# Degrees, row normalisation and table scaling of a graph layer, two stages written as one

## The chip, the cores and the metric

The kernel runs on one core of a Trainium2 chip. The metric is the device time of one execution in microseconds. The kernel computes one graph layer in stages that follow one another; this document is about two neighbouring ones.

## The reference, cut to what matters

12,500 nodes with 256 features, 200,000 weighted edges. The part that the change touches:

```python
xn = _layernorm(x, axis=-1)                     # (x - mean) / sqrt(var + 1e-5)
deg = segment_sum(ew_sl, row_sl, num_segments=N)   # edge weights by source node, self loops of weight 1
dinv = where(deg > 0, rsqrt(deg), 0.0)
norm = dinv[row_sl] * ew_sl * dinv[col_sl]
h7 = segment_sum((xn @ W)[col_sl] * norm[:, None], row_sl, num_segments=N) + b
...                                             # two dense layers on h7, an attention branch, a top-2 mixture of experts
```

The kernel gathers rows of a table `dinv * xn` first and multiplies by W afterwards. It also needs `xn` itself and `x + xn` (the skip rows). So between the sorting of the edges and the gathering stand: the weighted degree of each node, the normalisation of each row, and the scaling of each row by its node's `dinv`.

## The kernel before, in words

Nodes lie in 98 blocks of 128; a block of normalised rows is one 128 x 256 tile in `k.acc`, which holds all 98. An earlier phase has sorted the edges into 1664 tiles of 128 edges, each of which belongs to one block; a record is a packed word (target node, place of the source node within its block, `loc`) and the edge weight. Blocks are taken in order of their edge counts; `k.perm` says which block of nodes stands at place n, so SyncE loads one register of it for each DMA on x or the table (`natural`, line 182).

`degrees_and_rows` (from line 927) does two things side by side.

Its start (lines 1068 to 1101): SyncE loads the two halves of the records, VectorE adds them, TensorE turns them so that a tile's edges lie on partitions, ScalarE copies them to `k.recs`, and VectorE cuts `loc` out and splits the weight into three bf16 pieces whose sum is exact.

Then a loop of 13 trips of 128 tiles, in eight batches of 16. In each batch VectorE makes a one-hot of `loc` for each edge, 128 columns a tile (L1105, two instructions of 8 tiles), and TensorE multiplies: the one-hot as weights, the three pieces as three columns (L1177). After a trip the three columns are added (L1138), turned (L1163), copied (L1038) and added up by block with a matrix that says which tile belongs to which block (L1167). The total degree is complete when the last trip is through. The first trip and the last two are written out; trips 1 to 10 are a loop on the engines, in which addresses come from registers.

Beside each batch one block of x is normalised: SyncE loads it into a ring of four (L999), VectorE takes statistics (L1118, L1123), ScalarE the root (L1045), VectorE reciprocal and shift (L1128, L1130), and ScalarE writes `xn` to `k.acc` (L1048) and the skip rows to a ring of four (L1055). SyncE stores both (L1007, L1009) and loads the next block, all in one queue in program order. GpSimd only makes a row of numbers.

`scale_table` (from line 1192) begins after a barrier: roots and reciprocals of all 98 x 128 degrees, then ScalarE scales four and VectorE three of every seven blocks in `k.acc` in place (L1230, L1257), and SyncE stores each block to the table as soon as its seven are scaled (L1217), one register load and one DMA of 128 KB each. The bias of the layer is cut into three bf16 pieces beside it. `k.phase_done()` between phases clears the semaphores and makes all engines meet.

## Time and profile before

| | us |
|---|---|
| median of three runs (4654.85 to 4659.12) | 4658.87 |
| the profiled execution, its own time | 4660.25 |
| its span, first to last instruction | 4658.5 |
| the two stages: from the records' load to the gather stage's first instruction | 363.4 |

Over the whole span TensorE is busy 76%, VectorE 65%, GpSimd 58% and ScalarE 33%. The largest groups belong to the gather stage, which begins at 1166 us, and to the experts at the end. The page's forty slices are 116 us long; the two stages lie in slices seven to ten. A row of the timeline gives the start, the length of a merged run of equal instructions, the engine (SPq is SyncE's DMA queue), the line, what is written and read, the count, and in brackets the idle time before it and what ended that. Means in a row of groups are from start to write, and neighbours on one engine overlap by a part of it.

### The profile page before, as it was taken

To read this page: it belongs to the slowest core of one execution; us is meant where nothing else is said; L and a number is where in the kernel's file an instruction comes from. 1 tells how busy PE (TensorE), PEld (TensorE's weight loads), DVE (VectorE), ACT (ScalarE), POOL (GpSimd) and SP (SyncE) were. 2 spreads that over 40 slices of the span, in tenths; PEclk is the share of its full clock that TensorE was granted. 3 is DMA by queue.
4 is the path that set the end of the run, shared out by engine and by line. 5 is a ranking of instruction groups with operands and counts; after the bars stand their busy time and mean duration, and the time that the engine had idled before them with its cause. 6 is when DMAs were issued, how large, how long until landed. Compare 5 with 4: busy or idle time off the path is not lost. (4 is left out here: it accounts for less than half of the span.)

```text
span 4658.5 us, 80245 instructions
## 1 busy us (share of the span) xinstructions
PE 3532.4 (76%) x20196; PEld 2666.5 (57%) x20196; DVE 3032.5 (65%) x7684; ACT 1516.5 (33%) x4675; POOL 2709.1 (58%) x2419
## 2 busy tenths in 40 slices
PE   7777775791677777877765778777777679999986
PEld 6445543570344444444443666665666469999885
DVE  8899997883555655655554555555555675555566
ACT  2455553663111111111100322222222255555442
POOL 0488887000666666666666666666666325555553
PEclk9677787555888887888877888888898789999998
DMA  2111112454333333333333444444445712222456
GB/s 73 3 3 3 3 3 36 133 166 142 110 110 109 109 108 110 112 109 110 111 102 92 132 133 131 127 132 130 133 132 124 155 37 71 67 69 69 142 198 220
DMA packets 297683, 472.63 MB, mean 101 GB/s; under 512 B 97283, under 2 KB 195850, under 8 KB 297615
## 3 DMA queue, kind: packets, MB, share of 16 engines
q0 software_dynamic: 140544, 273.69, 23.8%
q1 hardware_dynamic: 149919, 194.17, 12.4%
q10 hardware_dynamic: 7154, 3.99, 0.3%
q8 instruction: 28, 0.46, 0.0%
q14 instruction: 38, 0.31, 0.0%
HBM read 350.37 MB, written 123.70 MB: 102 GB/s over the span
## 5 line engine op out<-in xcount | busy, mean ns | idle before, releaser
L1483 POOL DMA_INDIRECT rows<-table,idx x1664 | 1688.0, 1014 | 799.1 <-issue 466.4
L1764 DVE TENSOR_TENSOR acc<-acc,ps_seg 128x256 f32 x1664 | 697.1, 419 | 939.0 <-remote 669.2
L1929 PE MATMUL ps_seg<-rows,pick 128*128 128x256 f32 x3328 | 955.4, 419 | 129.6 <-issue 63.6
L1929 PEld LDWEIGHTS ps_seg<-rows,pick 128*128 128x128 f32 x3328 | 654.7, 208 | 355.1 <-issue 241.8
L756 POOL DMA_INDIRECT records<-sort_rec,sort_addr x280 | 527.6, 1884 | 262.0 <-DVE sort_rec L859 159.4
L1608 DVE TENSOR_SCALAR pick<-iota_row,loc,ewt 128x128 f32<-128x128 f32 x1680 | 530.3, 362 | 3.9
L1801 PE MATMUL ps_kv<-wkv,xT 128*128 128x512 f32 x392 | 264.5, 811 | 246.5 <-ACT xT L1506 149.1
L2367 POOL DMA_INDIRECT y_rows<-arena,idx x212 | 256.1, 1208 | 293.8 <-DVE arena L2414 235.7
L2499 PE MATMUL ps_h<-arena,up_now 128*128 128x128 f32 x3392 | 420.6, 278 | 0.0
L2483 PE MATMUL ps_y<-down_now,arena 128*128 128x256 f32 x1696 | 402.7, 381 | 0.0
L2499 PEld LDWEIGHTS ps_h<-arena,up_now 128*128 128x128 f32 x3392 | 401.2, 194 | 1.8 <-issue 0.3
L911 PE MATMUL ps_out<-acc 128*128 128x240 bf16 x1568 | 278.7, 362 | 143.7 <-DVE acc L845 143.6
L778 ACT ACTIVATE sort_others<-ps_rank,sort_own 128x98 f32<-128x98 f32 x840 | 272.9, 375 | 287.2 <-PE ps_rank L891 175.8
L2483 PEld LDWEIGHTS ps_y<-down_now,arena 128*128 128x128 f32 x1696 | 307.6, 191 | 33.3
L911 PEld LDWEIGHTS ps_out<-acc 128*128 128x128 bf16 x1568 | 200.8, 131 | 208.8 <-DVE acc L845 139.9
L2394 ACT ACTIVATE arena<-ps_h,up_now 128x128 f32<-128x128 f32 x848 | 241.7, 368 | 221.3 <-PE ps_h L2499 221.3
L2357 POOL DMA_INDIRECT arena<-ffn_rows,idx x212 | 223.7, 1055 | 141.9 <-DVE idx L2407 74.3
L1801 PEld LDWEIGHTS ps_kv<-wkv,xT 128*128 128x128 f32 x392 | 88.9, 243 | 343.6 <-issue 177.5
L2414 DVE TENSOR_TENSOR arena<-ps_y,down_now 128x256 f32<-128x256 f32 x212 | 90.0, 425 | 285.4 <-PE ps_y L2483 200.1
L2382 ACT ACTIVATE arena<-ps_x,gb 128x128 f32<-128x128 f32 x424 | 171.0, 453 | 208.5 <-issue 108.6
L1177 PE MATMUL ps_rows_tile_deg<-rows_ew,rows_at_node 128*128 (+1 forms) x1664 | 189.7, 180 | 49.6 <-DVE rows_at_node L1105 43.5
L845 DVE TENSOR_TENSOR acc<-sort_in_slot,sort_piece 128x3360 bf16<-128x3360 bf16 x112 | 208.8, 1907 | 7.0
(380 smaller groups left out, 5372.9 us busy)
## 6 DMA issues: line engine op xcount, KB each, us to landing
rows<-table,idx POOLq DMA_INDIRECT x1664
acc<-y_rows SPq DMA_DIRECT2D x28, 640.0 KB
rows_x<-in_x SPq DMA_DIRECT2D x100, 128.0 KB
xn<-xn_dram SPq DMA_DIRECT2D x100, 128.0 KB
xn_dram<-acc SPq DMA_DIRECT2D x98, 128.0 KB
skip_dram<-rows_skip SPq DMA_DIRECT2D x98, 128.0 KB
table<-acc SPq DMA_DIRECT2D x98, 128.0 KB
xT_dram<-xT SPq DMA_DIRECT2D x98, 128.0 KB
```

The source lines that it names most:

```text
L756: pool.indirect_dma_start(out=k.granules[h], out_offset=bass.IndirectOffsetOnAxis(addr[:, h, g:g + 1], 0), in_=rec[:, h, g * GRANULE:(g + ...
L778: last = act.activation(others[:, (m + h) % 2, :], ps_rank[g][:, at:at + BLOCKS], ACT.Relu, bias=own[:, :], accum_out=q[:, m:m + 1])
L911: last = pe.matmul(OUT, in_lane[:, h, c, :], valued[:, h, side, :, at, :], start=(c == 0), stop=(c == LOT - 1))
L1483: pool.indirect_dma_start(out=rows[:, t, :], out_offset=None, in_=k.table, in_offset=bass.IndirectOffsetOnAxis(idx[:, h, t:t + 1], 0), bou ...
L1608: dve.tensor_scalar(pick[:, h, t, :], k.iota_row[:, :], loc[:, h, t:t + 1], ewt[:, h, t:t + 1], ALU.is_equal, ALU.mult).then_inc(picked[t], 1)
L1764: dve.tensor_tensor(here, here, sums(u), ALU.add).then_inc(added[u], 1)
L1801: pe.matmul(ps_kv[:, :], xT[:, q, c, :], k.wkv[:, c, :], start=(c == 0), stop=False)
L1929: pe.matmul(sums(t), pick[:, h, t, :], rows[:, t, :], start=True, stop=True).then_inc(summed_up[t], 1)
L2367: pool.indirect_dma_start(out=k.y_rows, out_offset=bass.IndirectOffsetOnAxis(idx[:, u, 1:2], 0), in_=y[:, u % 2, :], in_offset=None, bound ...
L2394: act.activation(hT[:, slot, c * P:(c + 1) * P], ps_h[slot][:, c * P:(c + 1) * P], ACT.Gelu, bias=parts[slot][1][:, c:c + 1]).then_inc(gel ...
L2483: last = pe.matmul(ps_y[slot][:, 0:D], hT[:, slot, c * P:(c + 1) * P], parts[slot][2][:, c, :], start=(c == 0), stop=(c == HC - 1))
L2499: last = pe.matmul(ps_h[slot][:, c * P:(c + 1) * P], parts[slot][0][:, d, c * P:(c + 1) * P], xT[:, slot, d * P:(d + 1) * P], start=(d == ...
```

## The change

The two functions become one, `degrees_rows_table`, without a barrier between them, and no engine loops: everything is written out.

- Degrees. `loc` is cut into a high part (4 values) and a low part (32). For a group of 64 tiles VectorE makes one-hots of 4 columns and of 32, and multiplies the 4-column one by the three weight pieces, 12 columns a tile. TensorE takes the 32-column one-hot as weights and the 12 columns as the other operand: the result is 32 partitions x 12 columns a tile, in four PSUM banks, and VectorE adds the three pieces (`keep`). After two groups four small matmuls bring these 4 x 32 rows into the layout of 128 (`gather`), ScalarE copies them, and TensorE multiplies by that trip's tile-to-block matrix (`add`); VectorE adds the result to `deg`, which starts at 1.
- The tile-to-block matrices are made one trip at a time.
- Rows. Blocks are normalised in chunks of four: 25 chunks, x in a ring of three chunks, skip rows in a ring of two. `1/std + 1` is taken by VectorE instead of ScalarE. Two chunks are normalised before the records' copies, five more before the first group; group g then goes with chunk g + 7. Statistics are taken one chunk ahead.
- Table. As edges are sorted by block, the blocks up to `READY[j + 1]` have their whole degree after trip j. Their roots, reciprocals and scaling (half on ScalarE, half on VectorE) and their stores follow inside the loop, some six groups behind.
- SyncE: xn and skip rows are stored four blocks at a time; x and table still one block a DMA, with the registers of a chunk loaded by one instruction (`naturals`).
- The weight pieces are written twice each as pairs, by ScalarE instead of VectorE; the bias is cut at the very start.

Of the diff stand here the added lines that matter for the order of the work; what they replace is printed above, and is gone as a whole.

```diff
+            def naturals(eng, n, count):
+                _, values = nc.values_load_multi_w_load_instructions(
+                    k.perm[0:1, n:n + count], engines=[eng.engine], min_val=0, max_val=BLOCKS - 1,
+                    skip_runtime_bounds_check_because="blocks are numbered below BLOCKS")
+                return values
+            k.natural, k.naturals = natural, naturals
...
-                degrees_and_rows(k)
-                k.phase_done()
-                scale_table(k)
+                degrees_rows_table(k)
...
+    GROUP = P // 2
+    GROUPS_T = 2 * TRIPS
+    NORM = 4
+    NORMS = -(-BLOCKS // NORM)
+    LEAD = 7
+    EARLY = 2
+    X_CHUNKS = 3
...
+    HIGH, LOW = P // 32, 32
+    EW_PIECES = 3
+    WIDE = EW_PIECES * HIGH
+    HALF_BANK = GROUP // 2
+    READY = [BLOCKS * P * j // TILES_USED for j in range(TRIPS)] + [BLOCKS]
...
-        DEG = ps_deg[:, 0:BLOCKS]
+        DEG = [ps_T[r][:, 0:BLOCKS] for r in range(2)]
...
+                def load(c):
+                    for u, at in enumerate(k.naturals(sp, NORM * c, len(blocks_of(c)))):
+                        sp.dma_start(x[:, c % X_CHUNKS, u:u + 1, :], x_blocks[:, bass.ds(at, 1), :]).then_inc(
+                            x_in[c % X_CHUNKS], 16)
+                def put(c):
+                    b = blocks_of(c)
+                    start_after(sp, xn_out[c % X_CHUNKS], 16 * (c // X_CHUNKS))
+                    sp.wait_ge(xn_done, b.stop)
+                    sp.dma_start(xn_blocks[:, b.start:b.stop, :], k.acc[:, b.start:b.stop, :]).then_inc(xn_out[c % X_CHUNKS], 16)
+                    sp.wait_ge(skip_done, b.stop)
+                    sp.dma_start(skip_blocks[:, b.start:b.stop, :], skip[:, c % 2, 0:len(b), :]).then_inc(skip_out[c % 2], 16)
+                def put_table(j):
+                    at = k.naturals(sp, READY[j], len(ready(j)))
+                    sp.wait_ge(act_scaled, act_total(j))
+                    sp.wait_ge(dve_scaled, dve_total(j))
+                    for u, n in enumerate(ready(j)):
+                        sp.dma_start(table_blocks[:, bass.ds(at[u], 1), :], k.acc[:, n:n + 1, :]).then_inc(table_out, 16)
+                for c in range(X_CHUNKS):
+                    load(c)
+                sp.wait_ge(bias_cut, 2 * BIAS_PIECES)
+                sp.dma_start(k.bias3[:, :], pieces[0:1, :, :]).then_inc(bias_put, 16)
+                tabled = 0
+                for c in range(NORMS):
+                    put(c)
+                    if c + X_CHUNKS < NORMS:
+                        load(c + X_CHUNKS)
+                    g = c - LEAD
+                    if g >= 7 and g % 2 == 1:
+                        put_table(tabled)
+                        tabled += 1
+                for j in range(tabled, TRIPS):
+                    put_table(j)
...
+                def normalised(c):
+                    act.wait_ge(shift_done, c + 1)
...
+                    for u, n in enumerate(blocks_of(c)):
+                        act.activation(k.acc[:, n, :], x[:, c % X_CHUNKS, u, :], ACT.Identity, scale=rstd[:, n:n + 1],
+                                       bias=shift[:, n:n + 1]).then_inc(xn_done, 1)
+                    act.wait_ge(up_done, c + 1)
+                    start_after(act, skip_out[c % 2], 16 * (c // 2))
+                    for u, n in enumerate(blocks_of(c)):
+                        act.activation(skip[:, c % 2, u, :], x[:, c % X_CHUNKS, u, :], ACT.Identity, scale=up1[:, n:n + 1],
+                                       bias=shift[:, n:n + 1]).then_inc(skip_done, 1)
...
+                for c in range(EARLY):
+                    deviations(c)
+                    normalised(c)
                 for n, (w, g) in enumerate(turns):
                     act.wait_ge(turned, n + 1)
                     to = k.recs[:, g * P:span(g).stop * P, w]
                     act.activation(to if w == 0 else to.bitcast(F32), ps_T[n % 2][:, 0:P * len(span(g))],
                                    ACT.Identity).then_inc(unturned, 1)
+                act.wait_ge(unturned, len(turns))
+                piece(0, ew)
+                act.wait_ge(rest_done, 2)
+                piece(1, rest)
+                for c in range(EARLY, EARLY + 2):
+                    deviations(c)
+                act.wait_ge(rest_done, 4)
+                piece(2, rest2)
+                for c in range(EARLY, EARLY + 2):
+                    normalised(c)
+                for c in range(EARLY + 2, LEAD):
+                    deviations(c)
+                    normalised(c)
+                deviations(LEAD)
...
+                    if c + 1 < NORMS:
+                        deviations(c + 1)
+                    if g >= 3 and g % 2 == 1 and (g - 3) // 2 < TRIPS:
+                        keep_sums((g - 3) // 2)
+                    if g >= 5 and g % 2 == 1 and (g - 5) // 2 < TRIPS:
+                        roots((g - 5) // 2)
+                    if c < NORMS:
+                        normalised(c)
+                    if g >= 6 and g % 2 == 0 and (g - 6) // 2 < TRIPS:
+                        scaled((g - 6) // 2)
...
+                def moments(c):
+                    dve.wait_ge(x_in[c % X_CHUNKS], loads_of(c))
+                    for u, n in enumerate(blocks_of(c)):
+                        dve.bn_stats(stats[:, c % 2, u, :], x[:, c % X_CHUNKS, u, :]).then_inc(stats_done, 1)
+                    for u, n in enumerate(blocks_of(c)):
+                        dve.wait_ge(stats_done, n + 1)
+                        dve.bn_aggr(mv[:, c % 2, u, :], stats[:, c % 2, u, :]).then_inc(mv_done, 1)
...
                    dve.tensor_tensor(
+                        at_high[:, :, :].rearrange("p t (a two) -> p t a two", two=2),
+                        pairs(iota_b[:, 0:HIGH]).unsqueeze(1).to_broadcast([P, GROUP, HIGH // 2, 2]),
+                        high2[:, part, :].unsqueeze(2).to_broadcast([P, GROUP, HIGH // 2, 2]), ALU.is_equal).then_inc(high_done, 1)
+                    start_after(dve, tile_summed, g - 1)
+                    dve.tensor_tensor(
+                        at_low[:, r, :, :].rearrange("p t (c two) -> p t c two", two=2),
+                        pairs(iota_b).unsqueeze(1).to_broadcast([P, GROUP, LOW // 2, 2]),
+                        low2[:, part, :].unsqueeze(2).to_broadcast([P, GROUP, LOW // 2, 2]), ALU.is_equal).then_inc(low_done, 1)
+                    dve.wait_ge(high_done, g + 1)
+                    dve.tensor_tensor(
+                        weighted[:, r, :, :, :].rearrange("p t v (a two) -> p t v a two", two=2),
+                        at_high[:, :, :].rearrange("p t (a two) -> p t a two", two=2).unsqueeze(2).to_broadcast(
+                            [P, GROUP, EW_PIECES, HIGH // 2, 2]),
+                        ew3.unsqueeze(3).to_broadcast([P, GROUP, EW_PIECES, HIGH // 2, 2]),
+                        ALU.mult).then_inc(weighted_done, 1)
...
+                def keep(g):
+                    j = g // 2
+                    dve.wait_ge(tile_summed, g + 1)
+                    start_after(dve, gathered, j - 1)
+                    for q in range(2):
+                        at = g % 2 * GROUP + q * HALF_BANK
+                        dve.tensor_reduce(kept[:, j % 2, :, at:at + HALF_BANK],
+                                          ps_t[g % 2][q][0:LOW, 0:HALF_BANK * WIDE].rearrange(
+                                              "c (t v a) -> c a t v", v=EW_PIECES, a=HIGH), AX.X, ALU.add).then_inc(tile_kept, 1)
...
+                def scaled(j):
+                    dve.wait_ge(dinv_done, j + 1)
+                    stored(dve, j)
+                    for n in dve_share(j):
+                        dve.tensor_scalar(k.acc[:, n, :], k.acc[:, n, :], k.dinv[:, n:n + 1], None, ALU.mult).then_inc(dve_scaled, 1)
...
+                for g in range(GROUPS_T + 6):
+                    c = g + LEAD
+                    if c + 1 < NORMS:
+                        moments(c + 1)
+                    if g < GROUPS_T:
+                        one_hots(g)
+                    if 1 <= g <= GROUPS_T:
+                        keep(g - 1)
+                    if c < NORMS:
+                        inverses(c)
+                    if g >= 4 and g % 2 == 0 and (g - 4) // 2 < TRIPS:
+                        degrees((g - 4) // 2)
+                    if g >= 5 and g % 2 == 1 and (g - 5) // 2 < TRIPS:
+                        inverse_roots((g - 5) // 2)
+                    if g >= 6 and g % 2 == 0 and (g - 6) // 2 < TRIPS:
+                        scaled((g - 6) // 2)
+                    if g % 2 == 1 and g < GROUPS_T:
+                        blocks_of_tiles(g // 2)
...
+                def gather(j):
+                    pe.wait_ge(tile_kept, 4 * j + 4)
+                    start_after(pe, gathered_kept, j)
+                    for a in range(HIGH):
+                        last = pe.matmul(ps_d[:, a * LOW:(a + 1) * LOW], kept[:, j % 2, a, :], k.ident[0:LOW, 0:LOW],
+                                         start=True, stop=True)
+                    last.then_inc(gathered, 1)
+                def add(j):
+                    pe.wait_ge(gathered_kept, j + 1)
+                    pe.wait_ge(of_block_done, j + 1)
+                    start_after(pe, deg_added, j - 1)
+                    pe.matmul(DEG[j % 2], tile_degT[:, :], of_block[:, j % 2, :], start=True, stop=True).then_inc(block_summed, 1)
+                for g in range(GROUPS_T + 2):
+                    r = g % 2
+                    if g < GROUPS_T:
+                        pe.wait_ge(weighted_done, g + 1)
+                        pe.wait_ge(low_done, g + 1)
+                        start_after(pe, tile_kept, 2 * (g - 1))
+                        for t in range(GROUP):
+                            at = t % HALF_BANK * WIDE
+                            last = pe.matmul(ps_t[r][t // HALF_BANK][0:LOW, at:at + WIDE], at_low[:, r, t, :],
+                                             weighted[:, r, t, :, :].rearrange("p v a -> p (v a)"), start=True, stop=True)
                         last.then_inc(tile_summed, 1)
+                    if g >= 2 and r == 0:
+                        gather(g // 2 - 1)
+                    if g >= 3 and r == 1:
+                        add((g - 3) // 2)
```

## Rows read from the trace of the kernel before

**Rows 1.** Busy time by stretch: us; PE, PEld, DVE, ACT, POOL; PEclk, DMA share, GB/s
```profile
803.00:838.00 35.00, 6.07 (x28) 4.75 (x28) 21.06 (x30) 5.26 (x9) 0.00 (x0) 0.60 0.35 113
838.00:1066.00 228.00, 194.62 (x1601) 147.91 (x1601) 202.16 (x601) 157.51 (x401) 0.00 (x0) 0.50 0.52 167
1066.00:1082.00 16.00, 6.07 (x104) 4.66 (x104) 11.56 (x27) 4.26 (x13) 0.00 (x0) 0.50 0.08 26
1082.00:1166.00 84.00, 0.00 (x0) 0.00 (x0) 10.57 (x40) 20.22 (x51) 0.00 (x0) 0.50 0.45 153
...
806.00:814.00 8.00, 0.00 (x0) 0.00 (x0) 1.27 (x1) 0.00 (x0) 0.00 (x0) 0.50 1.09 354
```

**Rows 2.** Timeline at the seams: start us, us, engine, line, operation, count, idle before
```profile
802.70 1.31 SPq L997 DMA_DIRECT2D acc<-records  x2
...
1079.79 22.43 ACT L1230 ACTIVATE acc<-acc,dinv 128x256 f32<-128x256 f32 x56 [1.13 <-DVE dinv L1253]
1079.79 6.40 DVE L1257 TENSOR_SCALAR acc<-acc,dinv 128x256 f32<-128x256 f32 x24
1081.98 81.38 SPq L1217 DMA_DIRECT2D table<-acc  x98
...
1166.12 0.20 POOL L1470 MEMSET headmask<- 128x128 f32 x1 [363.25 <-POOLq L124]
```

**Rows 3.** Timeline of one-hots and tile matmuls, unrolled (845, 1065) and looped (933)
```profile
845.67 0.59 PE L1177 MATMUL ps_rows_tile_deg<-rows_ew,rows_at_node 128*128 128x3 bf16 x16 [1.50 <-DVE rows_at_node L1105]
...
933.41 9.13 PE L1177 MATMUL ps_rows_tile_deg<-rows_ew,rows_at_node 128*128 x64 [0.53 <-issue]
...
1065.92 7.30 DVE L1105 TENSOR_TENSOR rows_at_node<-rows_iota_b,rows_loc 128x1024 bf16<-128x1024 bf16 x12
```

**Rows 4.** Waits from 838 to 1066: who waited for whom, us, times, longest
```profile
DVE rows_at_node L1105 <- PE ps_rows_tile_deg L1177: 12.7, 42, 0.4
```

**Rows 5.** Register loads and table stores by line: ns min/median/max
```profile
L185 SPq TENSOR_LOAD <-perm x268: 218/270/505, 804.1 to 4621.8; - x134
...
L1613 DVEq TENSOR_LOAD <-places x104: 1096/1102/1405, 1168.4 to 3652.7; - x104
...
L1217 SPq DMA_DIRECT2D table<-acc x98: 340/340/353, 1082.0 to 1163.0; - x98
```

**Rows 6.** Groups by line and shape, 803 to 1166: count, busy us, mean ns, idle before
```profile
L1105 DVE TENSOR_TENSOR rows_at_node<-rows_iota_b,rows_loc 128x1024 bf16<-128x1024 bf16 x208 | 139.6, 676 | 20.0 <-PE ps_rows_tile_deg L1177 12.7 <-DVE rows_stats L1118 6.8
...
L1055 ACT ACTIVATE rows_skip<-rows_x,rows_mean_shift,rows_up 128x256 f32<-128x256 f32 x98 | 58.8, 600 | 5.0
L1118 DVE BATCH_NORM_STATS2 rows_stats<-rows_x 128x6 f32<-128x256 f32 x98 | 41.0, 418 | 1.3 <-issue 1.2
...
L1230 ACT ACTIVATE acc<-acc,dinv 128x256 f32<-128x256 f32 x56 | 22.4, 493 | 1.1 <-DVE dinv L1253 1.1
...
L1123 DVE BATCH_NORM_AGGREGATE rows_mv<-rows_stats 128x2 f32<-128x6 f32 x98 | 17.1, 175 | 0.0
...
L1257 DVE TENSOR_SCALAR acc<-acc,dinv 128x256 f32<-128x256 f32 x42 | 11.2, 344 | 0.0
...
L1138 DVE TENSOR_REDUCE rows_tile_deg<-ps_rows_tile_deg 128x128 f32<-128x384 f32 x13 | 7.2, 552 | 0.7 <-PE ps_rows_tile_deg L1177 0.7
```

**Rows 7.** The page's costliest groups: a wide VectorE product
```profile
L845 DVE TENSOR_TENSOR acc<-sort_in_slot,sort_piece 128x3360 bf16<-128x3360 bf16 x112 | 208.8, 1907 | 7.0
```

**Rows 8.** Timeline of SyncE, DMAs with fixed addresses
```profile
1166.12 1.78 SPq L1414 DMA_DIRECT2D xn<-xn_dram  x4
```

**Rows 9.** Timeline of the stage's start
```profile
804.75 6.76 SPq L999 DMA_DIRECT2D rows_x<-in_x  x4
...
815.04 3.63 DVE L1081 TENSOR_TENSOR acc<-acc 128x3328 f32<-128x3328 f32 x1 [7.77 <-DMA acc<-records]
...
819.89 0.63 ACT L1032 ACTIVATE recs<-ps_rows_T 128x512 int32<-128x512 f32 x1 [51.97 <-PE ps_rows_T L1155]
...
826.05 1.89 DVE L1090 CAST rows_loc<-rows_loc_all 128x3328 bf16<-128x3328 int32 x1 [3.09 <-ACT recs L1032]
```

More of the change, by code:

```diff
@@ new lines, in degrees_rows_table @@
+        guarded = sb("rows_guarded", [P, BLOCKS])
+        root = sb("rows_root", [P, BLOCKS])
+        inverse = sb("rows_inverse", [P, BLOCKS])
+        x = sb("rows_x", [P, X_CHUNKS, NORM, D])
+        skip = sb("rows_skip", [P, 2, NORM, D])
+        stats = sb("rows_stats", [P, 2, NORM, 6])
+        mv = sb("rows_mv", [P, 2, NORM, 2])
+        std = sb("rows_std", [P, 2, NORM])
+        rstd = sb("rows_rstd", [P, BLOCKS])
+        shift = sb("rows_shift", [P, BLOCKS])
+        up1 = sb("rows_up1", [P, BLOCKS])
```

413 lines of the change are left out of this document (164 added, 249 removed).

## The prediction

> **What bounds the kernel now.** I read the busy table and the forty slices first, then the stretches of the changed stages, the groups by line inside them, the waits, and the timeline at the seams. The chain that ended last, on the page, covers only the expert stage at the end and says nothing here; but every phase closes with a barrier of all engines, so a stage's full length stands in the total, and the question is what ends each of the two stages.
>
> The two stages run from 802.7 to 1166.1: 363.4 us, in which GpSimd idles [rows 1, 2]. Within it I see four stretches [rows 1]. From 803 to 838 the records are loaded, joined and cut. From 838 to 1066 the loop over 98 blocks takes 228 us, 2.33 us a block: VectorE is busy 202 of the 228 us, ScalarE 158, the DMA engines 52%. VectorE is the bound, and TensorE is just behind it: where the trips are unrolled, 16 tiles take 0.59 us; inside the hardware loop 64 tiles take 9.13 us, 0.143 us a tile or 2.28 us a batch, so VectorE also waits for TensorE there [rows 3, 4]. After 1066 come 16 us of left-over tiles, the degree's chain and the roots, and 84 us in which SyncE alone works: 98 table stores in 81.38 us, 0.83 us each, with the DMA engines 45% busy. ScalarE and VectorE finished their scaling long before [rows 1, 2]. The store is bound by SyncE's issue: a register load of 0.27 us and 0.34 us of DMA instruction, and some register work around them [rows 5]. DMA itself can do more: with the records' 1 KB rows it moved 354 GB/s [rows 1], against 167 and 153 in the loop and the stores.
>
> **How I price instructions.** Means overlap: 56 ScalarE scalings of mean 493 ns take 22.43 us, 0.40 each; 24 VectorE ones of 344 ns take 6.40, 0.27 each [rows 2, 6]. So back to back an instruction costs its mean less 0.08 or 0.09 us. For bf16 VectorE products, 1024 columns cost 0.61 back to back and 3360 cost 1.83: 0.52 ns a column and 0.07 fixed [rows 3, 7].
>
> **Change, VectorE.** Gone are 208 one-hots of 1024 columns: 208 x 0.61 = 127 us. A group of 64 tiles now costs 256, 2048 and 768 columns: 0.21 + 1.14 + 0.47 = 1.8 us, 26 groups 47 us. The nearest rows have pairs in long runs; the new patterns repeat a pair only twice, which no row shows, so the bound above is one column per 1.04 ns (twice as slow): 3.4 us a group; below, the mere column count at the wide rate, 1.6. I take 1.8. Two reductions of 384 columns: 1.0 us with the wait, from 0.55 mean [rows 6]. Statistics of four blocks: 4 x 0.34 + 4 x 0.10 + a wait = 1.9; the three small instructions for the chunk 0.5. Per two groups 0.5 (degrees), 0.45 (inverse), 0.5 (block of tiles), 1.0 (scaling). One group: 1.9 + 1.8 + 1.0 + 0.5 + 2.45/2 = 6.4 us while blocks are being normalised, 4.1 once they are through.
>
> **Change, ScalarE.** It keeps its two passes per block, 0.51 us each back to back (mean 0.60) [rows 6]; the 98 reciprocals-plus-one move to VectorE, the roots come by four: a chunk costs 8 x 0.51 + 0.3 = 4.4 us, and with half the scaling (1.9 blocks x 0.40) and the small steps about 5.5 a group. It is not the bound by itself.
>
> **Change, TensorE.** All of it is unrolled now: 64 tiles at the unrolled rate, at most 64 x 0.59/16 = 2.4 us a group, hidden under VectorE. Bounds: below 1.8 (narrower weights), above 9.1 at the looped rate [rows 3]; I take the unrolled row, which has the same kind of addresses.
>
> **Change, SyncE.** Register loads are gathered: one value 0.27, sixteen 1.10 us [rows 5], so 0.055 a further value and 0.44 for four, 0.65 for eight. A DMA with a register address then costs 0.83 - 0.27 - 0.05 = 0.51, one with a fixed address 1.78/4 = 0.45 [rows 2, 5, 8]. A chunk: two stores 0.9, four loads 2.5, and every second one 7.5 table stores 4.5; 5.7 us a group, below VectorE's 6.4. The Trainium skill, "Runtime: NRT & Kernel Launch", section Instruction fetch mechanics, puts a register load at some 200 ns per register even in bulk; by it four values would take 0.8 us and eight 1.6, and the stage would end about 5 us later. The row of 16 values in 1.10 us speaks against it, and the sum does not use it.
>
> **Change, DMA.** The bytes are the same, 51 MB for x, normalised rows, skip and table, but the 13 MB of the table lie in the loop: 2.1 MB a group. At 354 GB/s that is 5.9 us, just hidden; at the loop's present 167 it would be 12.5 us, and that is a rival below.
>
> **The wait that I expect to end last** in the main part is new. x lies in a ring of three chunks; a chunk's load is issued only after the stores of the chunk three before. VectorE starts a group with the statistics of the next chunk, so the circle runs: statistics to shift 5.2 us, ScalarE's eight passes 4.2, SyncE's skip store, register load and four loads 0.45 + 0.44 + 4 x 0.51 = 2.9, landing 1.6: 14.0 us for two groups, 7.0 each; the table stores that stand between the loads on SyncE add about 0.2. For the landing only bounds stand: all bytes of the last store plus the barrier took under 2.8 us (1163.4 to 1166.1) [rows 2], and nothing shows it below 1. So a group takes 7.2 us (6.8 to 7.8), and the three engines near it (6.4, 5.7, 5.9) fit under it. Behind the waiting statistics VectorE holds back the one-hots, and so TensorE.
>
> **The start of the stage** gets longer. As before SyncE's third DMA will be held until about 809 behind the records (its first four block loads took 6.76 us from 804.75, where three cost 2.4) [rows 9], the first chunks land near 815 to 818. VectorE takes two chunks' statistics ahead of the join: join done 823.5 instead of 818.7. ScalarE normalises those two chunks, 8.4 us to about 828.3, and TensorE's transposed records wait behind it; their copies took 819.9 to 826.0 before [rows 9], so now to 834. The three pieces in pairs are 3328 columns each on ScalarE, about 3.5 us (0.63 us for 512 columns in the copies, less fixed part [rows 9]), with VectorE's subtractions between: 846. Then five chunks at ScalarE's 4.4 and a small wait: group 0 starts at about 869, 31 us later than the first one-hot now, with 28 of 98 blocks done.
>
> **The sum.** 16 groups x 7.2 = 115: 984. Group 16 without a further load and group 17: 10.5, to 994.5. Eight groups x 4.1 = 33: 1027.5; SyncE has put away five or six of the 13 portions by then and 7 x 4.5 = 31.5 from about 1000, so it ends level. The last chain (reduction 1.0, gathering 0.8, copy 0.3, product 0.75, sum 0.4, root 0.3, inverse 0.4, four scalings 1.6, waits 1) 6.5: 1034. Eight table stores 4.1, landing and barrier 2.8: 1041, and 2 for what I have not listed: 1043. The stage ends 123 us sooner than at 1166.1. What I count at nothing: the bias pieces (2 us on VectorE, ahead of the x that it waits for), the second barrier (gone, in the sum already), and the stages after it, whose code and data are unchanged. 4660.25 - 123 = 4537 for the profiled execution, whose own time is 1.4 above the median of the three runs; 4537 is my figure.
>
> **Rivals.** (a) The two- and four-column patterns run at one column a cycle: +1.6 us a group; the circle becomes 15.6, 7.8 a group (+10 in the main part), the eight later ones +13: 4562. For it: no row has such short runs; against: the pairs of the present one-hots run at the wide rate. (b) Loads under mixed traffic land late, 5 us instead of 1.6: circle 17.4, 8.7 a group, +25: 4562; with some queueing of the table stores 4575. For it: a DMA was once held 4 us by a full queue; against: at most 1.5 MB are in flight. (c) TensorE does not keep the unrolled rate over long stretches and takes the looped 9.1 us a group: 26 x 9.1 = 237 from 869, 1106, and 14 at the end: stage 46 us shorter, 4614. Against it: each of the unrolled bursts in the trace took 0.59. The Trainium skill, "TensorE: Matmul & The Clock Gate", in the section Wait, 56ns, not 53.3ns, gives some 62 ns per matmul when the sequencer decodes it in software; with two instructions a tile that is 7.9 us a group and near this case, and the row of 0.59 us for 16 tiles disagrees. (d) The other side: slower. In both long stretches of this stage DMA moves 153 to 167 GB/s; if mixed loads and stores of 1 KB rows are limited near there, the 51 MB set the length. At 153 GB/s [rows 1] they need 335 us, with 12 for the records and 3 for the end 350, 13 us shorter than now; from 147 GB/s downward the change loses, and at 140 GB/s the stage takes 382, 19 us more: 4679. Against it: 52% busy engines, and 354 GB/s in the records' load. (e) The ring does not bind, VectorE does: 6.4 a group, -13, and a shorter start: 4518.
>
> **Chances.** My forecast with its own neighbourhood 4522 to 4555: 0.50; (e) 0.12; (a) 0.12; (b) 0.14; (c) 0.08; (d) 0.04, of which three quarters slower. Range 4510 to 4592: it holds all but (c), (d) and outliers, about 0.15. A change of under 0.2% (9 us) is what a measurement here cannot tell from none. Faster 0.95, same 0.02, slower 0.03.
>
> **What would show it.** The stage's length 240 us instead of 363; group starts 7.2 apart in the main part with VectorE's idle time ahead of the batch statistics, released by the DMA of x; 4.1 apart afterwards; one-hot means 0.3, 1.2 and 0.55 us; 64 matmuls in under 2.5 us; table stores 0.51 apart; the first one-hot near 869. If the statistics never wait, (e) or (a) holds; if TensorE ends the one-hots' waits, (c); if SyncE's DMA instructions themselves grow long, (d). A change outside the stage by more than 5 us would make the sum wrong in a way that I have no row for.

## The result and the profile after

The changed kernel takes 4550.71 us (median of 4 runs, 4548.52 to 4556.06) against 4657.65 for the kernel before (4 runs, 4654.85 to 4659.12) on the same chip: ratio 0.9772, 95% interval [0.9758, 0.9785], 107 us faster. The forecast was 4537, 14 us too low, inside its range.

The two profiled executions lie 111.4 us apart (4660.25 and 4548.86), since the one is above its median and the other below, and they say where the gain is. From the issue of the records' load to the next stage's first instruction the stage takes 253.1 us instead of 363.4 [rows 2], 110.3 less; what comes before it takes 800.25 us instead of 802.70, and what comes after it 3493.7 instead of 3492.4. Busy time of the changed kernel's stage in four stretches: up to the first group's one-hots, the 16 groups beside the normalising, groups 16 to 24, and the end (us; PE, PEld, DVE, ACT, POOL; PEclk, DMA share, GB/s):

```profile
800.00:871.00 71.00, 5.34 (x26) 4.26 (x26) 33.87 (x119) 44.50 (x80) 0.15 (x1) 0.55 0.66 219
871.00:990.50 119.50, 47.59 (x1094) 44.48 (x1094) 86.21 (x311) 76.97 (x174) 0.00 (x0) 0.50 0.73 240
990.50:1028.00 37.50, 27.55 (x619) 25.76 (x620) 35.60 (x99) 15.19 (x39) 0.00 (x0) 0.50 0.55 186
1028.00:1053.30 25.30, 6.51 (x83) 5.73 (x82) 9.28 (x31) 5.57 (x16) 0.00 (x0) 0.50 0.48 157
```

VectorE, busy 202 of 228 us in the old loop [rows 1], is busy 86 of 119.5 in the new main part: it has stopped being the bound there. It is the bound in the third line (35.6 of 37.5), and none of these engines is in the fourth. The groups by line in the whole stage (count, busy us, mean ns, idle before) answer to [rows 3, 6]:

```profile
L1354 PE MATMUL ps_rows_tile<-rows_weighted,rows_at_low 128*32 128x12 bf16 x1664 | 48.7, 173 | 120.8 <-DVE rows_weighted L1252 120.8
L1247 DVE TENSOR_TENSOR rows_at_low<-rows_iota_b,rows_low 128x2048 bf16<-128x2048 bf16 x26 | 31.7, 1219 | 0.0
L1252 DVE TENSOR_TENSOR rows_weighted<-rows_at_high,rows_ew 128x768 bf16<-128x768 bf16 x16 | 8.8, 552 | 0.0
L1242 DVE TENSOR_TENSOR rows_at_high<-rows_iota_b,rows_high 128x256 bf16<-128x256 bf16 x26 | 7.0, 268 | 0.0
```

The 139.6 us of one-hots [rows 6] have become 31.7 + 7.0 and 14.3 of weighting (16 products here and 10 more of the same size with 5.5 us), 53 us. TensorE waits for VectorE, no longer the other way round. Who waited in the main part (us in total, times, longest):

```profile
DVE rows_stats L1165 <- DMA rows_x<-in_x: 32.0, 11, 5.1
ACT acc L1093 <- DVE rows_shift L1177: 26.1, 15, 2.8
ACT rows_std L1085 <- DVE rows_mv L1168: 17.8, 8, 3.5
```

That is the circle through the ring of three, and the timeline shows one whole turn of it (start us, us, engine, line, operation, count, idle before):

```profile
910.98 1.41 DVE L1165 BATCH_NORM_STATS2 rows_stats<-rows_x 128x6 f32<-128x256 f32 x4 [3.42 <-DMA rows_x<-in_x]
...
915.56 0.15 DVE L1177 SCALAR_TENSOR_TENSOR rows_shift<-rows_mv,rows_rstd 128x4 f32<-128x4 f32 x1
915.75 2.07 ACT L1093 ACTIVATE acc<-rows_x,rows_shift,rows_rstd 128x256 f32<-128x256 f32 x4 [2.75 <-DVE rows_shift L1177]
...
917.73 2.06 ACT L1098 ACTIVATE rows_skip<-rows_x,rows_shift,rows_up 128x256 f32<-128x256 f32 x4
...
919.82 0.35 SPq L1048 DMA_DIRECT2D skip_dram<-rows_skip  x1
...
920.66 1.92 SPq L1039 DMA_DIRECT2D rows_x<-in_x  x4
...
924.73 1.40 DVE L1165 BATCH_NORM_STATS2 rows_stats<-rows_x 128x6 f32<-128x256 f32 x4 [2.08 <-DMA rows_x<-in_x]
```

From the waiting statistics at 910.98 to the next that wait for the same queue, at 924.73, are 13.75 us in four pieces: 4.8 to ScalarE's first pass, 4.1 of passes, 2.8 on SyncE (919.82 to 922.58), 2.15 from the last issue to the landing. Then the first table stores come, and the same SyncE must carry them:

```profile
929.50 2.08 ACT L1093 ACTIVATE acc<-rows_x,rows_shift,rows_rstd 128x256 f32<-128x256 f32 x4 [2.76 <-DVE rows_shift L1177]
929.95 3.92 SPq L1055 DMA_DIRECT2D table<-acc  x7
...
933.97 0.41 SPq L1046 DMA_DIRECT2D xn_dram<-acc  x1
934.42 0.55 SPq L1048 DMA_DIRECT2D skip_dram<-rows_skip  x1
935.96 2.34 SPq L1039 DMA_DIRECT2D rows_x<-in_x  x4
...
940.76 1.41 DVE L1165 BATCH_NORM_STATS2 rows_stats<-rows_x 128x6 f32<-128x256 f32 x4 [3.21 <-DMA rows_x<-in_x]
```

The chunk's normalised rows were ready at 931.6 (929.50 + 2.08) and its skip rows at 933.5; their stores went out at 933.97 and 934.42, because SyncE was issuing seven table stores. The loads behind them are late by as much. Pairs of groups without table stores take 13.3 to 14.4 us, those with them 15.2 to 16.8.

At the end of the stage the engines have finished long before SyncE:

```profile
1037.83 1.71 ACT L1145 ACTIVATE acc<-acc,dinv 128x256 f32<-128x256 f32 x4 [0.82 <-DVE dinv L1293]
...
1053.40 0.20 POOL L1571 MEMSET headmask<- 128x128 f32 x1 [252.97 <-POOLq L121]
```

```profile
1004.28 46.53 SPq L1055 DMA_DIRECT2D table<-acc  x61
```

The last scaling ends at 1039.5; SyncE works through 61 stores from 1004.3 to 1050.8 and hardly waits for anybody. That is 0.76 us a store, where one store behind another costs 0.52. Two things make the difference (ns: least, median, most; the first row is of the whole stage, the second of these 61 stores):

```profile
L187 SPq TENSOR_LOAD <-perm x38: 296/840/2890, 801.6 to 1044.7; - x38
L1055 SPq DMA_DIRECT2D table<-acc x61: 340/340/1699, 1004.3 to 1050.5; - x61
q8 instruction: 4, 0.07, 0.7%
```

The seven gathered register loads between the portions take 9.7 us together. And three of the 61 store instructions, at 1007.98, 1022.84 and 1030.81, take 1.51, 1.70 and 1.38 us instead of 0.34, 3.6 us more. Each of the three begins within 0.2 us of a 16 KB packet of the queue that the profile calls "instruction" (third row: four such packets between 1004 and 1051, at 1007.9, 1015.2, 1022.7 and 1030.7). The other three table stores of this kernel that took over 0.7 us (at 946.2, 962.4 and 978.7) also lie within 0.6 us of one. That fetches of instructions hold them is therefore likely, but no run here tests it.

### The profile page after: what moved, and what is told of

Read it like the earlier page. It is cut to its first block and busy times, and to the rows that moved or that the text cites. A ratio compares the mean times of both kernels' runs of the same rounds, so it can differ in the third digit from the quotient of the medians.

```text
span 4547.1 us, 77334 instructions
## 1 busy us (share of the span) xinstructions
PE 3408.5 (75%) x20283; PEld 2585.4 (57%) x20283; DVE 2944.6 (65%) x7545; ACT 1473.8 (32%) x4511; POOL 2724.2 (60%) x2419
## 5 line engine op out<-in xcount | busy, mean ns | idle before, releaser
L2528 DVE COPY down_now<-down_all 128x1280 f32 x212 | 175.3, 827 | 48.3 <-DVE arena L2515 21.9
```

## The experiments

Each is the changed kernel with one edit, unless it says more. Stage lengths are read from one profiled execution each. The runs were made on several chips; on all but the one named below the kernel before takes 4657 to 4659 us. The rest of the kernel, which no edit touches, took 3485 to 3504 us there, so differences of under 20 us are read from the stage alone. "Main" is from the first one-hot of group 0 to that of group 16, "late" from 18 to 25, "end" from 25 to the end; the changed kernel has 119.6, 27.5 and 25.5.

**Four buffers for x.** One buffer of kept sums instead of two and small tiles of the degree that share their place make the room, and the weight pieces of one more group lie in `k.acc`.

```diff
-    X_CHUNKS = 3
-    FIRST_GROUPS = 10
+    X_CHUNKS = 4
+    FIRST_GROUPS = 11
...
-        kept = sb("rows_kept", [LOW, 2, HIGH, P])
+        kept = sb("rows_kept", [LOW, 1, HIGH, P])
```

> The changed kernel with x in a ring of four chunks instead of three (room for it from the degree's small tiles, which share one, and from one buffer of kept sums instead of two). In the changed kernel the stage takes 253.0 us and its 16 main groups 119.7, 7.5 each. Theory A (the circle statistics, passes, stores, next load over three chunks ends last): the load has a whole group more, VectorE's 6.4 us or SyncE's work becomes the bound, main groups 6.4 to 6.9, stage 10 to 16 us shorter, total near 4537. Theory B (VectorE's work sets the length): nothing, 4551. Theory C (the loads land when the DMA engines let them): 0 to 3 us less.

Measured: 4533.02 us (4 runs, 4526.75 to 4538.47), ratio to before 0.973 [0.9706, 0.9753]. Main 96.5, 6.0 us a group; stage 233.2, 20 us shorter. VectorE's wait for x in the main part (866.1 to 962.6 here) falls from 32.0 us to

```profile
DVE rows_stats L1163 <- DMA rows_x<-in_x: 9.4, 5, 3.2
```

and the first group starts 66.7 us after the records' load instead of 70.6. But the end grows from 25.5 to 30.1: what is scaled sooner queues longer on SyncE. The ring was the bound, and taking it away earned more than I thought, since VectorE's own work is under my 6.4. What waiting is left stands where table stores are in SyncE's queue: the last three pairs take 14.1 to 14.3 us, those before them 9.8 to 11.7.

**1/deviation ahead of the one-hots.** The piece "statistics to shift" holds 1.8 us of one-hots and 1 us of reductions that have nothing to do with it; the edit puts the shift ahead of the next chunk's statistics as well.

```diff
                 for g in range(GROUPS_T):
...
+                    if c < NORMS:
+                        inverses(c)
...
-                    if c < NORMS:
-                        inverses(c)
```

> The changed kernel with one order changed on VectorE: reciprocal and shift of chunk c stand ahead of the statistics, one-hots and reductions of the same group instead of behind them. Work and loads are the same. Theory A: the circle loses the statistics, one-hots and reductions that stood ahead of the shift, at least 3 us in two groups, main groups 6.4 to 6.8, stage 10 to 16 us shorter, total 4535 to 4541. Theory B: nothing, VectorE has as much to do. Theory C: nothing.

Measured: 4539.83 us (4 runs, 4538.16 to 4543.62), ratio 0.9751 [0.9728, 0.9773]. Main 109.3, the wait for x 22.1 us in the main part, stage 241.5. The first piece of the turn is now "statistics to root", since ScalarE takes the next chunk's root ahead of its passes:

```profile
894.65 1.40 DVE L1165 BATCH_NORM_STATS2 rows_stats<-rows_x 128x6 f32<-128x256 f32 x4 [1.00 <-DMA rows_x<-in_x]
896.37 0.30 ACT L1085 ACTIVATE rows_std<-rows_mv,eps 128x4 f32<-128x4 f32 x1 [1.74 <-DVE rows_mv L1168]
896.57 2.06 ACT L1093 ACTIVATE acc<-rows_x,rows_shift,rows_rstd 128x256 f32<-128x256 f32 x4
```

It is 1.9 us instead of 4.8. A shorter step of the circle shortens the circle: the main part gains 10.3 us, and VectorE has as much work as before. The gain is not even. The first four pairs of groups take 46.4 us instead of 55.4, the last four, with table stores in SyncE's queue, 62.9 instead of 64.2: there the stores decide, and the order on VectorE hardly matters.

**The one-hot of 32 columns made twice.**

```diff
+                    for again in range(2):
+                        start_after(dve, low_done, 2 * g + again)
                         dve.tensor_tensor(at_low[:, r, :, :] ...
```

> The changed kernel with the one-hot of 32 columns made twice, the second over the first: 1.14 us more on VectorE in each of the 26 groups. Theory A: half of it counts in the main part, since the circle spans two groups, 16 x 0.57 = 9, and the later groups hide it behind SyncE's stores: stage 9 to 12 us longer. Theory B: all of it counts, 26 x 1.14 = 30 us.

Measured: 4568.98 us (1 run). Main +8.7, groups 16 and 17 +1.6, late +8.9, end +1.4, stage 274.3, 21 us longer and between A's 9 to 12 and B's 30. Of 1.22 us more work a group, 0.54 show in the main part (the rest fits into the wait for x) and all of it in the late groups. A had the main part right; that SyncE's backlog would hide the late groups was wrong, for these are VectorE's.

**All table stores behind the last chunk's stores.**

```diff
-                    if g >= 7 and g % 2 == 1:
-                        put_table(tabled)
-                        tabled += 1
```

> The changed kernel with all table stores behind the last chunk's stores on SyncE, as a part of the change undone: none inside the main part. Theory A: the pairs of groups that had a portion of stores in them become about 1.2 us shorter each (6 us in all), and SyncE stores 98 blocks at 0.78 us from about 995: the stage ends near 1074, 20 us longer. If instead the scaling on VectorE and ScalarE ends the stage and SyncE keeps up at 0.51 us a block, the end is near 1050 and nothing changes.

Measured: 4577.07 us (1 run). Main 111.9, 13.99 us a pair, which is the circle with no table stores in it; the end 52.4, stage 273.1. So the table stores cost the main part 7.7 us, and overlapping them is still worth 20.

**Single register loads.**

```diff
-                    at = k.naturals(sp, READY[j], len(ready(j)))
...
-                        sp.dma_start(table_blocks[:, bass.ds(at[u], 1), :], ...
+                        sp.dma_start(table_blocks[:, bass.ds(k.natural(sp, n), 1), :], ...
```

> SyncE fetches each place of x and of the table by a load of one register just ahead of its DMA, in place of one load of 2 to 8 registers ahead of them all. Theory A (a gathered load of n registers is what SyncE pays for with 0.7 to 2.9 us, and 32 singles between the issues cost no more than it): the stage within 4 us of the changed kernel's 253. Theory B (a load has a fixed cost of about 0.25 us and each further register little, so that gathering earns something and the 0.7 to 2.9 us of the long ones have another cause): 94 further loads at 0.25 to 0.3 us, some 24 us more on SyncE, of which the circle of x takes 4 loads a pair, about 1 us, so 8 us in the 16 main groups, and the last chain about 14 us more; stage 270 to 278.

Measured: 4575.12 us (2 runs, 4571.47 to 4578.77). Stage 271.8: first group +3.6, main +11.0, end +4.1. A load of one register takes

```profile
L182 SPq TENSOR_LOAD <-perm x266: 13/271/895, 802.5 to 4540.4; - x133
```

0.27 us and a store with it 0.82. Gathering earns 18.7 us: the total is near B, but not its parts, for it expected 14 us at the end and 8 in the main part. But the gathered loads of 7 and 8 values near the stage's end took 1.65, 0.72, 0.76, 1.20, 1.86, 1.68 and 1.86 us, and B has no cause for them. In three other kernels of this study in which SyncE's program there is the same (the one-hot made twice, made four times, the stores behind) the same seven loads had the same lengths within 0.07 us, whether SyncE had been waiting before them or not. So it isn't the traffic of the moment. On GpSimd's queue (two experiments further down) the last six portions have the same order of lengths, 0.59, 0.61, 1.21, 2.21, 2.05 and 2.27 us, so it goes with the portion as well as with the place in SyncE's program; what it is stays open.

**ScalarE's queue stores its own blocks from portion 6 on.**

```diff
+                def act_puts(j):
+                    at = k.naturals(act, READY[j], len(act_share(j)))
+                    act.wait_ge(act_scaled, act_total(j))
+                    for u, n in enumerate(act_share(j)):
+                        act.dma_start(table_blocks[:, bass.ds(at[u], 1), :], k.acc[:, n:n + 1, :]).then_inc(act_table_out, 16)
```

> From portion 6 on ScalarE's queue stores the half of the table blocks that ScalarE itself scaled; SyncE stores only VectorE's half. Theory A (from group 18 on SyncE is late by its own stores, and the last one leaves it 11 us after the last scaling): the 16 main groups hardly change (within 2 us of 119.6), and from group 25 on 25.5 becomes 15 to 17; stage 242 to 246, total 4539 to 4543. Theory B (the end of the stage is set by ScalarE's scaling and by the DMA queues): ScalarE has to issue 3 to 4 stores of 0.5 us and a register load of about 1 us before it may scale the next portion, so what SyncE saves ScalarE adds; stage 250 to 256, total as the changed kernel's.

Measured: 4537.94 us (4 runs, 4533.36 to 4552.06), ratio 0.9743 [0.9721, 0.9765]. End 19.2 instead of 25.5, main 120.6, stage 248.6. From the last chunk on SyncE issues 36 stores where it issued 61, and it pauses for the scaling. The end is now the last chain and ScalarE's own three steps: scaling until 1044.1, four stores until 1046.2, landing and barrier until 1049.9:

```profile
1042.36 1.71 ACT L1148 ACTIVATE acc<-acc,dinv 128x256 f32<-128x256 f32 x4 [0.47 <-DVE dinv L1305]
1044.24 1.95 ACTq L1154 DMA_DIRECT2D table<-acc  x4
1049.92 0.20 POOL L1583 MEMSET headmask<- 128x128 f32 x1 [248.44 <-POOLq L121]
```

**The one-hot of 32 columns made four times**, `range(4)` in the edit above: as many one-hot columns a group as the kernel before wrote for 64 tiles.

> The one-hot of 32 columns is made four times, so that VectorE writes 32,768 columns a group of it as the kernel before wrote 8 tiles of 128 columns four times over; its output is the same. Theory A (the circle of 14 us per two groups holds only as long as VectorE needs under 7 a group; three more one-hots of 1.22 us put it at 6.4 + 3.7 = 10.1): 16 main groups 161 us, groups 16 to 18 +7, late groups 3.9 + 3.7 = 7.5 each, stage 253 + 42 + 7 + 26 + 2 = 330, total 4627. Theory B (the circle and VectorE's work add up, as the wait stands between them): 3.7 us on each of 26 groups, stage 253 + 95 = 348.

Measured: 4618.18 us (2 runs, 4617.97 to 4618.39). Main 149.8, 9.4 a group; late 54.1, 7.7 each; stage 319.5. The wait for x has nearly gone from the main part (872.4 to 1022.2 here):

```profile
DVE rows_stats L1165 <- DMA rows_x<-in_x: 2.2, 3, 1.4
```

The two costs don't add up (B is out by 28): the wait hides work until VectorE needs the circle's 7 us. A was 11 us too high in the main part, by my VectorE price of 6.4. The run also splits the change's gain: with the old number of columns 44 of the 110 us are left, and the narrower one-hots are worth the other 66. Scaling and storing beside the loop and TensorE's unrolled rate are in the 44; no run divides them, except that overlapping the stores is worth 20 by the experiment above.

**Ring of four, 1/deviation first, x's register load ahead of the wait for the normalised rows, and two queues, in one kernel.**

> Four buffers for x (one kept buffer and shared statistics columns make the room), 1/deviation ahead of the group's one-hots, x's register load ahead of the wait for the chunk's normalising, and ScalarE's queue for its own table blocks from portion 6 on. Theory A (each step of the circle and the tail's queue is a cost of its own): main groups at VectorE's pace, 6.0 each as with four buffers alone or just over it; the end from group 25 on 30.1 with four buffers becomes about 18; stage 233 - 12 = 221, total 4521 or, if the 10 us longer rest that the run with four buffers showed belongs to it, as the kernel with four buffers less 12. Theory B (with four buffers VectorE and the DMA engines are the bound to the end): stage 229 to 235, total within 5 us of four buffers alone (4533).

Measured: 4517.54 us (5 runs, 4512.27 to 4523.77), ratio 0.9699 [0.9684, 0.9714]. Main 93.9, late 27.6, end 19.2, stage 222.3. A has it: its figures were 96, 18 and 221 for main, end and stage, and 4521 in all. In the main part two groups still take 10.1 and 9.8 us instead of 6; in the last kernel below, where SyncE has no table stores there, they take 6.2 each.

**All table stores on GpSimd's queue.**

```diff
             @block.gpsimd
...
+                for j in range(TRIPS):
+                    at = k.naturals(pool, READY[j], len(ready(j)))
+                    pool.wait_ge(act_scaled, act_total(j))
+                    pool.wait_ge(dve_scaled, dve_total(j))
+                    for u, n in enumerate(ready(j)):
+                        pool.dma_start(table_blocks[:, bass.ds(at[u], 1), :], k.acc[:, n:n + 1, :]).then_inc(table_out, 16)
```

> All 98 table stores and their register loads go from SyncE's queue to GpSimd's, which has nothing else in this stage; the rest is as in the changed kernel. Theory A (SyncE's stream is the bound where the table stores stand in it: 7.7 us in the main groups by the run with the stores behind, about 9 at the end by the 11 us that the last store leaves SyncE after the last scaling): main groups 112, from group 25 on 25.5 becomes 15 to 17, stage 234 to 238, total 4531 to 4535. Theory B (the late landings of x and the end are the DMA engines' share, not the issue): as many bytes in less time, stage 248 to 256. Theory C (a DMA with a register address costs GpSimd over 1 us, as its gathers cost it 1.0 us apart in the next stage): 7.5 stores of 1.2 us are 9 of the 7.8 to 15 us of a portion, and the last portion alone is 9 us in place of 5: from group 25 on 20 to 24, stage 240 to 246.

This and the next kernel ran on another chip, on which the kernel before takes 4371.09 us (9 runs) at a granted clock of 0.87 to 0.88 in place of 0.83. Measured: 4269.02 us (4 runs, 4264.54 to 4276.24), ratio 0.9767 [0.9752, 0.9783], no better than the changed kernel's. Main 115.3, end 36.9, stage 261.2, longer than any of the three theories has it. The stores are issued 0.61 us apart, so C's 1.2 is wrong. But it was right that GpSimd is the worse queue at the end, and the cause is twofold: a gathered register load takes 0.6 to 4.9 us on it (median 2.3), and long after its last store the stage is not over:

```profile
L187 POOLq TENSOR_LOAD <-perm x13: 591/2269/4865, 801.9 to 1044.3; - x13
```

```profile
1047.32 4.81 POOL L1069 DMA_DIRECT2D table<-acc  x8 [2.45 <-issue]
1063.11 0.20 POOL L1563 MEMSET headmask<- 128x128 f32 x1 [10.98 <-POOLq L121]
```

```profile
L1031 POOLq COMPARE_BRANCH  x1: 38/38/38, 1053.6 to 1053.6; - x1
L1031 POOLq DRAIN  x1: 8069/8069/8069, 1053.8 to 1053.8; - x1
```

These are 11.0 us from the end of the last issue to the next stage, against 2.6 from SyncE's (1050.8 to 1053.4). The landing isn't late: GpSimd is past its wait for all table stores at 1053.6, 1.5 us after the last issue. What follows is one DRAIN instruction of 8.07 us, with which GpSimd's program of this stage closes, and then the barrier. In the main part nobody waits for the table, and there it costs nothing; the gain of 4.3 us is less than the 7.7 of A.

**The same with four buffers, 1/deviation first and the early register load.**

> The version with four buffers for x, 1/deviation first and x's register load ahead of the wait, but all table stores on GpSimd's queue in place of SyncE's and ScalarE's. Theory A (VectorE now sets the main groups, at 5.9 in the version with two queues, and the last chain sets the end): main groups 92 to 95, groups 16 to 18 from 11.2 to 8 (no backlog of table stores ahead of x), late groups 27.5, from group 25 on 15 to 19, total 4510 to 4518 against the 4517.5 of two queues. Theory C (GpSimd's issue is dear): from group 25 on 22 or more, total 4520 to 4526.

Measured, on that other chip: 4247.31 us (5 runs, 4229.62 to 4249.76), ratio 0.9708 [0.9689, 0.9727]. Main 86.5, groups 16 and 17 8.1, late 27.6, end 36.9, stage 229.4. Main better than A's 92 to 95, the end as C says, with the same DRAIN of 8.07 us in it (from 1021.5). The totals of A and C were for the first chip and can't be compared.

**GpSimd's queue for portions 0 to 4, SyncE's for 5, SyncE's and ScalarE's from 6 on**, with the other three edits.

> The version with four buffers for x and two queues, with the stores of portions 0 to 4, which fall into the main groups, on GpSimd's queue; portion 5 is SyncE's, and from portion 6 on SyncE and ScalarE share as before. The three queues' runs so far are taken to add up stage by stage (theory A): main groups 86.5 and groups 16 to 18 8.1 as with all stores on GpSimd, late groups 27.6, from group 25 on 19.2 as with two queues; stage 70.3 + 141.4 = 212, 10 us under the version with two queues (222.3), so 4507.5 against its 4517.5 where the kernel before takes 4657. Theory B (the late part only takes what the main part gives, since ScalarE and the DMA engines are loaded in it): from group 25 on 24 to 28, stage 217 to 221, total 4513 to 4517.

Measured: 4505.2 us (5 runs, 4497.65 to 4511.19), ratio 0.9676 [0.9663, 0.969]: the fastest, about 45 us under the changed kernel. Main 86.5, 8.1, late 27.7, end 19.2, stage 210.7; the parts added up as A took them to. GpSimd's last store is issued at 955.6, long before the end, so its DRAIN (3.09 us here) costs nothing. Its main part:

```profile
869.70:956.20 86.50, 47.58 (x1094) 44.47 (x1094) 85.12 (x312) 76.30 (x174) 20.12 (x37) 0.50 0.99 328
```

VectorE is busy 85.1 of 86.5 us and no longer waits for x at all, so a fifth buffer has nothing to gain. The DMA engines are 99% busy at 328 GB/s, and SyncE feels it: a load of x takes it 0.72 us to issue at the median, where the changed kernel's takes 0.34. A second bound is near, then; no run shows which would hold first if VectorE had less to do.

```profile
L1039 SPq DMA_DIRECT2D rows_x<-in_x x57: 332/722/2020, 869.8 to 950.9; - x57
```

## Why the prediction was right, and where its 14 us went

The stage was to take 240.3 us from the records' load and takes 253.1, 12.8 more. The rest of the account is small: 1.3 us more after the stage, 2.4 less before it, and a median 1.9 above the profiled execution. By the steps of the sum, counted from that load:

| step | predicted | measured |
|---|---|---|
| first one-hot of group 0 | 66.3 | 70.6 |
| 16 main groups | 115 (7.2 each) | 119.6 (7.5 each) |
| groups 16 and 17 | 10.5 | 9.9 |
| 7 groups, 18 to 24 | 28.7 (4.1 each) | 27.5 (3.9 each) |
| group 25, last chain, stores, landing, 2 in reserve | 19.5 | 25.5 |

**The mechanism was right.** The predicted wait is there in name and size: the circle was put at 14.0 us and is 13.75 in its clean turn, 13.99 a pair without table stores. Its pieces were put at 5.2, 4.2, 2.9 and 1.6 and measured 4.8, 4.1, 2.8 and 2.15, so errors of both signs cancel in the sum. More buffers, a shorter piece, and more work on the engine that waits all did what a circle says.

**"The table stores that stand between the loads add about 0.2"** was the mis-sized term of the main part. I counted one part of their issue; they hold back the chunk's own two stores as well, and with them the loads: 2 us a pair in the last four pairs, 7.7 us in all by the experiment. First pairs at 13.9 us instead of 14.4 paid for some of it.

**"SyncE ends level"** was the step that failed at the end. A portion was priced at 4.5 us, 7.5 x 0.51 and 0.65 for the register load. SyncE did begin its last eight portions about when I said, at 1004, and at my price it would have been through at 1040; it was through at 1050.8. From 1004.3 on it took 10.8 us more than priced: 5.2 in the seven register loads, 0.72 to 1.86 us each for 7 or 8 values, 3.6 in the three store instructions that were held, and 2 in small steps. I had one portion of stores, 4.1 us, between the last scaling and the last issue, and there are 11.3. Two queues gave 6.3 us of it back. The page of the Trainium skill that I set aside, "Runtime: NRT & Kernel Launch", section Instruction fetch mechanics, says about 200 ns per register even in bulk: 1.86 us for eight is 0.23 each and agrees, 0.72 is 0.09 each and does not; over the seven loads, 53 values in 9.7 us, it is 0.18. It also put the stage's end about 5 us later, and 6.0 was missing, though the register loads are only a part of that. The row that I held against it, 16 values in 1.10 us [rows 5], is of VectorE's queue, and I used it for SyncE's without a reason.

**The first group** came 4.3 us later than worked out. I had the ring bind only from group 0 on, but it binds already here: the statistics at the head of group 0 wait for x,

```profile
869.24 1.41 DVE L1165 BATCH_NORM_STATS2 rows_stats<-rows_x 128x6 f32<-128x256 f32 x4 [3.31 <-DMA rows_x<-in_x]
```

and with four buffers and nothing changed in VectorE's order the first group came 3.9 us sooner.

**VectorE's price** was too high: 6.4 a group, where the fastest version runs at 5.8 once all of its work is there (6.2 and 5.4 in turn) and at 3.7 to 5.1 in the first groups, which have no blocks to scale yet; 5.4 is the mean. It did not matter behind the circle. It is a reason why the ring of four took 23 us from the main part and not 13, the figure of rival (e).

The rivals: (a), one column a cycle, is out: the 2048 columns of the new short patterns took 1.219 us, 0.60 ns each with everything fixed in it, where (a) has over 1. Less the 0.08 of overlap that is the priced 1.14. (b) was half there: x landed 2.15 us after its last issue, not 5, but the queueing that it named is real. (c), TensorE at 9.1 us a group, is out: 64 matmuls take 1.87 us, 29 ns each. The 62 ns that the Trainium skill gives in "TensorE: Matmul & The Clock Gate", section Wait, 56ns, not 53.3ns, for decoding without the hardware decoder are not seen with 12 columns and a weight load of 32 each. (d), slower by DMA, is out: 240 GB/s in the main part, and 328 in the fastest version. (e), a ring that doesn't bind, is out by VectorE's 32.0 us of waiting for x.

## What to carry to other kernels

When several engines pass buffers round a ring, add up one whole turn, the DMA landing and the queue's issue included, and divide by the groups per turn; if that is above every engine's own work, the cheapest gains are another buffer and moving foreign work out of a step of the turn. A queue that issues for two purposes delays the urgent one by the whole burst of the other: give bulk stores that nobody waits for to an idle queue, and take the quickest queues for the last ones. Before GpSimd's queue gets the last stores of a stage, look at what its program does behind them: here 8 us passed after they had landed. Price an instruction on the engine that issues it; a gathered register load cost 0.07 us a value on VectorE's queue and 0.09 to 0.41 on SyncE's.

## What the runs showed of the hardware

- A gathered register load has no one price. On SyncE in the changed kernel 4 values took 0.30 to 1.1 us, 2 values 1.61 and 7 to 8 values 0.7 to 2.9; on GpSimd's queue 7 to 8 values took 0.6 to 6.9 in two kernels, while a single one is 0.27 at the median on SyncE. The lengths of the last seven portions come again within 0.07 us in three other kernels with the same instructions there.
- A store instruction of SyncE that takes 0.34 us took 0.8 to 1.9 six times in 98, each time within 0.6 us of a 16 KB packet of the instruction queue.
- A plain store with a register address is issued every 0.61 us by GpSimd and every 0.52 us by SyncE. After GpSimd's last one 11.0 us pass until the next stage, 8.07 of them in one DRAIN instruction, after SyncE's 2.6. With 37 stores instead of 98, issued earlier, the DRAIN took 3.09 us.
- The DMA engines moved 328 GB/s of mixed loads and stores, in packets of 1 and 4 KB, at a busy share of 0.99, twice what the old loop had [rows 1]. Nobody waited for a landing of x, but SyncE's issue of a load grew from 0.34 to 0.72 us at the median.
- Chips differ: the same kernel before takes 4657 us on one and 4371 on another, at mean granted clocks of 0.834 and 0.871 to 0.880. The difference is not in this stage, where the granted clock is 0.50, the lower level of 1.2 GHz, on both. The records' load began at 801.9 us there, with all table stores on GpSimd's queue, and at 800.3 here, in the changed kernel; the part after the stage took 3206 us at a granted clock of 0.94 there and 3494 us at 0.87 here.
